# First attention step in halves, in a new order on every engine, and the fourth supergroup's results read by ScalarE's queue

## The reference

```python
def gnn(h, adj, W_w, W_b, a):                       # h = layernorm(x)
    Wh = h @ W_w + W_b
    e = leaky_relu((Wh @ a[:128])[:, None] + (Wh @ a[128:])[None, :], 0.2)
    attention = softmax(where(adj > 0, e, NEG), axis=1)     # adj: 4096 x 4096, int32
    return attention @ Wh
x = x + gnn(layernorm(x), adj, W_w, W_b, a)
scores = layernorm(x) @ Wg.T + bg                   # top 2 of 8, softmax of the two
out = x + sum over e of combine[:, e] * (relu(z @ W1[e].T + b1[e]) @ W2[e].T + b2[e])   # z = layernorm(x)
```

## Time and profile before

| | us |
|---|---|
| median of 3 runs | 419.58 (419.39 to 420.35) |
| the profiled execution's own time | 420.92 |
| its span in the profile | 419.2 |
| PE busy | 388.5 |
| DVE busy | 295.4 |
| ACT busy | 270.4 |
| POOL busy | 202.3 |

### The profile page before, as it was taken

How to read it: one execution, slowest core, us unless ns; L and a number is a source line. 1 busy time by engine, 2 the same in 40 slices (tenths; PEclk the granted TensorE clock), 3 DMA queues, 4 the chain that set the end, 5 groups by cost and what they waited for, 6 DMA issues and landing times.

```text
span 419.2 us, 8413 instructions
## 1 busy us (share of the span) xinstructions
PE 388.5 (93%) x2434; PEld 260.0 (62%) x2434; DVE 295.4 (70%) x816; ACT 270.4 (65%) x451; POOL 202.3 (48%) x247
## 2 busy tenths in 40 slices
PE   1699999999999999999899999999989999999960
PEld 1445555445444445444356667798879999999960
DVE  5878697998899988799988698258951593111173
ACT  1577889837767865895267785357646677667630
POOL 3364331200041485303772238779788777555560
PEclk9859999999999999999999999999999999999995
DMA  6999788878968899989566994766667777677695
GB/s 198 366 394 331 256 325 288 346 320 295 373 285 290 305 356 356 378 316 318 195 201 248 354 352 156 232 193 205 225 224 232 236 232 251 220 227 245 221 380 189
DMA packets 45612, 116.46 MB, mean 278 GB/s; under 512 B 7517, under 2 KB 19682, under 8 KB 38902
## 3 DMA queue, kind: packets, MB, share of 16 engines
q1 hardware_dynamic: 37494, 100.81, 67.8%
q0 software_dynamic: 4320, 8.47, 6.2%
q10 hardware_dynamic: 3744, 6.56, 5.2%
HBM read 84.57 MB, written 13.07 MB: 233 GB/s over the span
## 4 chain that ended last, share of the span: by engine, by line
PE 66%; DVE 9%; ACT 8%; issue 7%; DMA 5%; SPq 4%; POOL 2%; ACTq 0%; POOLq 0%; DVEq 0%
PE acc L1567 37%; PE acc L1669 9%; DVE prob L953 5%; ACT G_all L1334 4%; PE yt L1669 3%; PE hps L1651 3%; PE hps L1653 3%; PE hps L1652 3%; DMA adj<-adjT 3%; PE yt L1612 2%; PE pj L1688 1%; PE pj L1528 1%; DMA adj<-ybuf 1%; SPq L546 1%; POOL ybuf L804 1%
## 5 line engine op out<-in xcount | busy, mean ns | idle before, releaser
L1567 PE MATMUL acc<-prob,Wh 128*128 128x512 f32 (+1 forms) x576 | 240.3, 558 | 5.6 <-DVE Wh L892 3.1
L953 DVE SCALAR_TENSOR_TENSOR prob<-s_bc,E_col,G_all 128x1024 f32<-128x1024 f32 (+2 forms) x160 | 170.1, 1091 | 24.2 <-PE acc L1567 19.7
L1567 PEld LDWEIGHTS acc<-prob,Wh 128*128 128x128 f32 x576 | 105.3, 193 | 102.1 <-issue 87.6
L1334 ACT ACTIVATE G_all<-adj 128x2048 bf16<-128x2048 int32 (+1 forms) x67 | 118.9, 1800 | 21.7 <-DMA adj<-adjT 10.9
L788 POOL DMA_INDIRECT xbuf<-xr,slot x64 | 72.4, 1132 | 49.5 <-PE acc L1567 31.6
L804 POOL DMA_INDIRECT ybuf<-wst,dest x71 | 73.7, 1037 | 46.3 <-ACT wst L1417 25.3
L1669 PE MATMUL acc<-wall,prob 128*128 x368 | 51.0, 282 | 0.0
L1669 PEld LDWEIGHTS acc<-wall,prob 128*128 128x128 f32 x368 | 44.7, 192 | 0.1
L1205 DVE COPY share<-slab 128x1 f32<-128x1 f32 x45 | 6.8, 153 | 50.3 <-DMA slab<-xbuf 46.7
L1407 ACT ACTIVATE prob<-hps 128x512 f32<-128x512 f32 x46 | 27.6, 599 | 6.5 <-PE hps L1653 1.4
L698 POOL TENSOR_TENSOR scratch<-scratch,mhalf 128x4 f32<-128x4 f32 x8 | 13.2, 1646 | 31.0 <-DVE scratch L877 31.0
(11 more groups left out here) (245 smaller groups left out, 554.6 us busy)
## 6 DMA issues: line engine op xcount, KB each, us to landing
adj<-adjT SPq DMA_DIRECT2D x52, 1024.0 KB, 7.4
adj<-adjT SPq DMA_DIRECT2D x16, 768.0 KB, 6.7
s_bc<-wall SPq DMA_DIRECT2D x47, 256.0 KB
wlb<-wall SPq DMA_DIRECT2D x24, 256.0 KB
slab<-xbuf SPq DMA_DIRECT2D x71, 65.0 KB
adj<-ybuf SPq DMA_DIRECT2D x6, 512.0 KB, 7.1
xs<-x SPq DMA_DIRECT2D x8, 256.0 KB, 10.0
wst<-wcat ACTq DMA_DIRECT2D x8, 256.0 KB, 4.1
```

The source lines that it names most:

```text
L953: nc.vector.scalar_tensor_tensor(prob[n % PR][:, 0:w], c_bc[:, P * AT[g]:P * AT[g] + w], E_col[:, u:u + 1], G[m % GR][:, k * w:(k + 1) * w ...
L1334: nc.scalar.activation(G[m % GR][:, 0:w], adj_sb[m % AR][:, 0:w], ACT.Relu).then_inc(s_G, 1)
L1567: last = nc.tensor.matmul(bank[:, 0:k * P], Wh[:, u, :], prob[n % PR][:, b * P:(b + k) * P], start=(u == 0), stop=(u == TILES - 1), skip_g ...
```

## The change

On DVE, step 0 becomes `first_step`: each half (512 columns) of the row is clipped as soon as ACT has made it, and its scores follow at once; the first half's scores have a semaphore of their own (`s_Pa`). Of `Wh` only tile 0 is scaled ahead of the scores, tiles 1 to 3 behind them. The statistics of group 2 are split: `moments(2)` moves ahead of the wait for POOL's `reach`, `variances(2)` behind the first step; `stats(3)` moves behind `weigh(2)`. On ACT `keep_E(0)` moves ahead of `keep_s(1)`, and `keep_E(1)` ahead of the conversion of chunk 2 and of `normalise(2)`. On PE `project(0)` moves ahead of `project_s(1)`, `project(1)` waits for `s_ED` and no longer stands behind `transposes(2)`, which moves from step 1 to step 3, with `project(2)` and `project_s(2)` from step 3 to step 4. At the end, the reads of pieces 6 to 8 move from SP's queue to ACT's.

```diff
@@ SP: last_reads @@
-                for c in range(SOON):
-                    store(c)
-                given_back(OLDER)
-                for c in range(SOON, LATER):
-                    read_back(c)
-                for c in range(SOON, len(last_pass)):
+                for c in range(len(last_pass)):
                     store(c)
@@ DVE @@
-            def stats(i):
+            def moments(i):
+                dve.wait_ge(s_xin[i], 16)
+                for u in range(GT * i, GT * (i + 1)):
+                    last = nc.vector.bn_stats(st0[:, u, :], xs[:, u, :])
+                return mark(last)
+
+            def variances(i, moments_made):
                 mine = range(GT * i, GT * (i + 1))
-                dve.wait_ge(s_xin[i], 16)
-                for u in mine:
-                    last = nc.vector.bn_stats(st0[:, u, :], xs[:, u, :])
-                link(last)
+                after(moments_made)
                 for u in mine:
                     last = nc.vector.bn_aggr(mv0[:, u, :], st0[:, u, :])
...
+            moments_2 = moments(2)
             dve.wait_ge(s_reach, 1)
...
             nc.vector.tensor_scalar(G[0][:, :], adj_sb[0][:, :], 0.0, None, ALU.max).then_inc(s_G0, 1)
-            stats(2)
...
+            def first_step():
+
+                clipped = []
+                for h in range(2):
+                    cols = slice(GW * h, GW * (h + 1))
+                    dve.wait_ge(s_sbc, h + 1)
+                    clipped.append(mark(nc.vector.tensor_scalar(c_bc[:, cols], c_bc[:, cols], 1.0, None, ALU.min)))
+                    if h == 0:
+                        dve.wait_ge(s_ED, 1)
+                        nc.vector.tensor_scalar(Wh[:, 0, :], Wh[:, 0, :], w_col[:, 0:1], None, ALU.mult)
+                        dve.wait_ge(s_G0, 1)
+                    after(clipped[h])
+                    nc.vector.scalar_tensor_tensor(prob[0][:, cols], c_bc[:, cols], E_col[:, 0:1], G[0][:, cols],
+                                                   op0=ALU.max, op1=ALU.min).then_inc(s_Pa if h == 0 else s_P, 1)
+                nc.vector.tensor_tensor(Wh[:, 1:GT, :], Wh[:, 1:GT, :],
+                                        w_col[:, 1:GT].unsqueeze(2).broadcast_to([P, GT - 1, F]),
+                                        ALU.mult).then_inc(s_whs, 1)
...
-                        i = group_at(n, -7, 4)
+                        i = 3 if n == -2 else group_at(n, -7, 4)
                         if i is not None:
                             stats(i)
...
-                group_row(0)
-                weigh(0)
-                keep_Wh(0, False)
-                stats(3)
+                first_step()
+                variances(2, moments_2)
                 main(False)
@@ ACT @@
-                        i = group_at(n, -1)
+                        if n == -2:
+                            keep_E(1)
+                        i = 2 if n == -1 else group_at(n, -1, 3)
                         if i is not None:
                             normalise(i)
...
-                        if n == -1:
-                            keep_E(1)
...
                 keep_s(0, False)
+                keep_E(0)
                 keep_s(1, False)
-                keep_E(0)
                 main(False)
...
-            for r in range(YR):
-                act.wait_ge(s_sc[r], 16 * len(range(r, NT, YR)))
-            for c in range(LATER, len(last_pass)):
-                u, k = last_pass[c]
-                nc.scalar.dma_start(landed(u, k), yv[:, u:u + k, :, :]).then_inc(s_yl[c], 16)
+            for tiles, reads in ((OLDER, range(SOON, LATER)), (NT, range(LATER, len(last_pass)))):
+                for r in range(YR):
+                    act.wait_ge(s_sc[r], 16 * len(range(r, tiles, YR)))
+                for c in reads:
+                    u, k = last_pass[c]
+                    nc.scalar.dma_start(landed(u, k), yv[:, u:u + k, :, :]).then_inc(s_yl[c], 16)
@@ PE @@
             project_s(0)
+            project(0)
             project_s(1)
-            project(0)
...
-                pe.wait_ge(s_P, n + 1)
-                if u % GT == 0 and g == 0:
-                    pe.wait_ge(s_whs, u // GT + 1)
-                if n == 0:
-                    pe.wait_ge(s_sbc, 2)
+                if n or general:
+                    pe.wait_ge(s_P, n + 1)
+                    if (u % GT == 0 or n == 1) and g == 0:
+                        pe.wait_ge(s_whs, u // GT + 1)
                 for h, (bank, b, k) in enumerate(halves(g)):
+                    if n == 0 and not general:
+                        pe.wait_ge(*((s_Pa, 1) if h == 0 else (s_P, 1)))
+                    if n == 0 and h == 1:
+                        pe.wait_ge(s_sbc, 2)
...
-                        i = group_at(n, 1)
+                        if n == 1:
+                            project(1)
+                        i = 2 if n == 3 else group_at(n, 1, 3)
                         if i is not None:
                             transposes(i)
-                        if n == 1:
-                            project(1)
-                        i = group_at(n, 3)
+                        i = 2 if n == 4 else group_at(n, 3, 3)
                         if i is not None:
                             project(i)
```

More of the change, by code:

```diff
@@ L1519, in transposes, with project @@
                 last.then_inc(s_t0, 1)
-            def project(i):
+            def project(i, general=False):
                 pe.wait_ge(s_hT, i + 1)
-                ge(pe, s_whs, i)
+                if i == 1 and not general:
+                    pe.wait_ge(s_ED, 1)
+                else:
+                    ge(pe, s_whs, i)
                 if i == 0:
```

16 lines of the change are left out of this document (9 added, 7 removed).

## The result

| | before | after |
|---|---|---|
| median of the runs shown | 419.49 us (419.26 to 421.3, 6 runs) | 414.62 us (413.42 to 415.87, 6 runs) |
| ratio to before, 95% interval | | 0.9874 [0.9849, 0.99] |
| the profiled execution | 420.92 us, span 419.2 | 415.07 us, span 413.5 |

The change takes 1.26% off, 4.9 us between the medians and 5.85 us between the two profiled executions.

What follows compares the result with a forecast made beforehand. PE was taken to bound the kernel, busy 99.93 of 100 us in the attention steps. Gains of 2.0 us early and 1.1 at the end, 3.1 in sum, took 419.58 to 416.5 us, range 414.0 to 418.7.

Steps and rivals of the forecast that it cites:

- The early part: First steps on PE: earlier start and fewer waits, 2.4 us before the clock, taken as 2.0 us (1.0 to 3.0).
- The end: Last reads: pieces 6 to 8 issued earlier from ACT's queue let DVE finish sooner, 1.1 us (0.5 to 1.6).
- the forecast case: Whole kernel: both the early gain and the end gain come, giving 415.0 to 418.0 us; chance 0.48.
- the second rival: Early steps: the clock stays up or rises early, giving 412.5 to 415 us; chance 0.15.
- The way to the first step: PE's start of step 0: first half of scores ready at 16.95, start at 17.0 instead of 19.30, 2.3 us earlier.
- The statistics ahead of the flag: DVE before the wait for reach: moved statistics cost 0.87 us, taken as 0 delay, up to 0.87 without cover.
- The next steps: PE's second step and transposes(2): the 0.43 us wait goes, and the second step's scores are ready 1.2 us early.
- The wait that is added: ACT's keep_E(1) waits for the projection ahead of chunk 2's conversion: costed at 0, some 0.7 us at full clock.
- the low stretch ends at 27.5: Early PE clock: rising as long after the second step's start as before, it gives 2.1 us back, about 3.8 in all.
- The sum of the steps: Early PE steps added up before the clock: 2.3 + 0.43 - 0.35 = 2.4 us.
- A wait between 25 and 100 us: Sign against the prediction: PE gathering new waits between 25 and 100 us would show it wrong.
- its three reads go out at 405.5: Kernel's end: ACT issues its three reads at 405.5 to 406.8 instead of 409.30 to 410.59, right after its last operation.

Runs made afterwards that it cites:

- the kernel with early filler: Changed kernel plus 12 unused transposes ahead of TensorE's first wait and 9 ahead of the first real transposes: 415.41 us, ratio 0.9897.
- the kernel before with filler: Kernel before, order untouched, plus 12, 9, 24 and 20 unused transposes in TensorE's early idle stretches: 418.4 us, ratio 0.9983.
- The filled kernels: Kernels with unused TensorE transposes in idle stretches: kernel before 418.4 us, step 0 in one piece 416.72 us, the old order with halves 420.87 us.
- chip A: One of three sets that each ran on one chip; the kernel before ran beside it, 29 runs, median 420.18 us.
- the old order with halves: Changed kernel with transposes(2), project(2), project_s(2) and keep_E(1) put back in their old places, step 0 still halved: 420.66 us, ratio 1.0023.
- step 0 in one piece: Changed kernel with step 0 not halved, waiting for the whole row and making 1024 scores at once, new order kept: 419.05 us, ratio 0.9966.

## Why the prediction was right, and where its sizes were off

416.5 us were predicted, in 414.0 to 418.7; it is 414.6. The sign holds, and so does the mechanism for holes and waits. The early part, put at 2.0 us with the clock in it, was far too small: PE's lead is 5.93 us at 32 us and 5.05 at the last scatter. The end, put at 1.1, was too large. And 414.6 lies outside the forecast case (415.0 to 418.0) and inside the second rival (412.5 to 415, chance 0.15), in which the clock rises early; the range holds it only because it took in half of that rival. The base is in part luck as well: the six runs of the kernel before in the result all lie at 419.26 us and above, and from its upper group the change takes 2.2 us, not 4.9.

- **The way to the first step.** Forecast 17.0, measured 17.45. The order of events is as written, but the clock was at its lower level there in the profile after, so the wide passes took 2.05 and 1.96 and not 1.3 and 0.9. The hole of 0.35 is 0.27.
- **The statistics ahead of the flag**, costed at 0: held. ACT's first half of the row is at 14.29 (14.31 before).
- **The next steps**: no wait ahead of the second step or the transposes in this profile, as written (0.23 us ahead of the second step in the other).
- **The wait that is added**, costed at 0 with 0.7 for the range: the conversion of chunk 2 stands at 22.18, and PE doesn't wait. With an earlier clock it does: 0.69 and 1.54 us in the kernel with early filler.
- **The clock is what was mis-sized in the 2.0 us.** They were 2.4 for the holes and waits less 0.4 for the clock. The 2.4 was near: 2.01 by the kernel before with filler. The step that failed is "the low stretch ends at 27.5", and 31.8 as its other end: it ended at 20.0 in one profile of the changed kernel and at 18.5 in the other, and the clock didn't fall again before the end. So the clock gave back time, where it was booked as a small loss. The profile of before shows one execution; I carried its moments of rise and fall over to a kernel in which they needn't be the same. That the three timed runs had their clocks up sooner isn't shown either: 419.4 to 420.4 us is where the lower group lies. Measured in one way (the kernel before with filler, against its own profile), the clock is 3.9 of the 5.9 us; in another (the two groups of the kernel before), 3.65 us lie between them with no edit at all, though no run of the upper group was profiled, so that the clock in the first 32 us parts them is read from its mean alone. The changed kernel's 414.6 is 2.2 below the one group and 5.8 below the other. The medians of the filled kernels return less, 1.35 and 2.3 us and in one nothing, so the exact share stays open. The second rival gave 35.6 for the end of the seventh step; it is 35.65, but part of that is chance, for the rival had PE bound by the other engines there, and PE waits for none. Its price of 412.5 wasn't reached, for it counted the end's 1.1 and no loss between.
- **The sum of the steps was right only as a sum.** I priced halves and order as adding up. Against the median of chip A each alone gives between 0.5 us more and 1.1 less time, both together 5.7 less (without the edit at the end): a hole that either leaves costs its own length and what the clock loses behind it.
- **A wait between 25 and 100 us**, named as what would show me wrong, came: 1.38 us at 80.5. It took 1.3 of the 5.93 us in this execution. DVE's scaling of `Wh` at 72.69 took 1.77 us in place of 0.69 while POOL's own operation on two tiles ran beside it; that the one slowed the other was not tried.
- **The end, 1.1 us**: 0.2 to 0.3 by the groups, and nothing by the kernel without it (414.44 us, with the change's early part alone, for 414.62). The step that failed is "its three reads go out at 405.5": ScalarE needed 3.9 us from its last operation to the first read, the way out of its branch to the common code, where I had it ready at once. The trace of before has the same: its last operation ends at 405.39, and its first wait of the common code stands at 409.22. And when that was taken away nothing came of it: the transfers took as much longer. That points to the transfers as what paces the end; no run here takes them apart further. The doubt from the Trainium skill (DMA: Bandwidth & Descriptors, Rules for kernel authors), that another queue gives no bandwidth, was the better guide: the three reads landed in 4.2 us from SP's queue (early part only) and in 3.7 from ACT's, and those issued sooner, at 400.30, took 7.2.

## What to carry to other kernels

A hole on TensorE of 3 to 4 us, as here, is to be priced twice: its length, and double time for the work behind it. Even one of 2.05 us was followed by 3.4 us at half clock. Two edits that each close one of two such holes may show nothing apart and all of it together, so try them together before dropping either. Where a kernel's own runs form two groups, compare group with group: a median of twelve can move by 1 us on the mix alone.

## What the runs showed of the hardware

- The same program has two groups of runs, 416.8 us at a mean clock of 0.984 and 420.4 at 0.973 (23 and 55 runs). The changed kernel, without the long hole, has one; but so has the old order with halves, which has the longest hole (eleven of twelve runs at 0.973 to 0.975), so a hole alone doesn't make two. The Trainium skill (TensorE: Matmul & The Clock Gate, Part 1: The HAM clock gate) says that the phase differs from run to run, and these runs agree. It also puts the penalty of the ramp below 1% of a typical span; the 3.65 us between the groups are 0.9% of 420.
- The record of the granted clock starts with its first change: at 14.7 us in the profile of before, 20.0 in that of the changed kernel, 29.7 in that of step 0 in one piece. A span that begins at half clock is listed as full until then, and its mean clock comes out higher than that of a faster run (0.989 at 419.05 us, 0.986 at 415.07). The same turns the groups of step 0 in one piece round: 419.3 us at 0.989, 417.4 at 0.977.
- From ScalarE's compare-and-branch at the end of its branch to the first instruction of the common code it took 4.0 us (399.91 to 403.91), and 2.9 to 5.2 over the thirteen traces of kernels whose reads stand there. With the reads inside the branch the first wait follows at once (at 398.6, with its last operation at 398.57).
